# One finishing stage by blocks of token slots, and a pipelined table stage with the edge index in it

## The reference

```python
def _forward(x, edge_index, W_gat, att_src, att_dst, b_gat, ln_gamma, ln_beta, W1, b1, W2, b2):  # x = layernorm(t2)
    h = (x_flat @ W_gat).reshape(M, HEADS, NUM_EXPERTS)              # 4 heads x 4 experts
    src, dst = edges and one loop (m, m) per token
    e = leaky_relu(a_src[src] + a_dst[dst], 0.2)
    ee = exp(e - segment_max(e, dst)[dst])
    alpha = ee / (segment_sum(ee, dst)[dst] + 1e-16)
    agg = segment_sum(h[src] * alpha[:, :, None], dst) + b_gat
    scores = _layernorm(agg, ln_gamma, ln_beta).mean over heads      # 4 scores per token
    topk_s, topk_i = top_k(scores, 2); w = softmax(topk_s)
    for ei in range(4):
        out = out + g_ei[..., None] * (gelu(x @ W1[ei] + b1[ei]) @ W2[ei] + b2[ei])
    return out
# result: t2 + out
```

## Time and profile before

| | us |
|---|---|
| median of 3 runs | 6876.4 |
| lowest and highest | 6873.09, 6878.02 |
| the profiled execution | 6868.53 |
| its span | 6867.0 |
| DVE busy in the span | 3009.2 (44%) |
| POOL busy | 3021.5 (44%) |
| PE busy | 2998.4 (44%) |
| POOL's 2048 gathers of the edge stage, busy | 2008.8 |

### The profile page before, as it was taken

The page is one execution under the profiler, slowest core; times in us unless marked ns, Lnnn a source line. Parts: engine busy times, 40 slices in busy tenths (PEclk is TensorE's granted clock), DMA queues, the critical chain, the costliest instruction groups (busy, mean ns, idle before and its releaser), DMA issues. The chain is left out here.

```text
span 6867.0 us, 61389 instructions
## 1 busy us (share of the span) xinstructions
PE 2998.4 (44%) x16592; PEld 2106.3 (31%) x16592; DVE 3009.2 (44%) x4102; ACT 1471.6 (21%) x5678; POOL 3021.5 (44%) x3316
## 2 busy tenths in 40 slices
PE   2888888879999450000444231313121131314400
PEld 1444454468888340000333120202111120203200
DVE  5888888559999321011999020201111020202229
ACT  0333333468888220000000010100000010101100
POOL 1000000046767237776000767575757667572345
PEclk9788888779999555555555555555555555555555
DMA  6666666556666331000000011111111111111125
GB/s 138 89 92 94 96 95 96 83 90 102 103 101 102 87 91 8 9 7 7 3 4 3 13 46 16 33 24 33 28 32 25 15 46 15 34 24 47 49 70 198
DMA packets 584829, 385.88 MB, mean 56 GB/s; under 512 B 404739, under 2 KB 531507, under 8 KB 581715
## 3 DMA queue, kind: packets, MB, share of 16 engines
q1 hardware_dynamic: 385528, 221.54, 14.5%
q10 hardware_dynamic: 89403, 109.89, 9.2%
q0 software_dynamic: 109728, 52.69, 6.6%
HBM read 235.34 MB, written 147.70 MB: 56 GB/s over the span
## 5 line engine op out<-in xcount | busy, mean ns | idle before, releaser
L1483 POOL DMA_INDIRECT e_row<-scratch_table,e_edge x2048 | 2008.8, 981 | 990.0 <-issue 681.8
L1664 PE MATMUL f_psY<-f_w,f_hid 128*128 128x64 f32 x1568 | 363.1, 425 | 1649.5 <-ACT f_hid L1615 1052.8
L1547 DVE TENSOR_TENSOR f_y<-f_psY,f_b 128x1024 f32<-128x1024 f32 x49 | 59.8, 1220 | 2294.7 <-DMA scratch_vpad<-v 1432.9
L1664 PEld LDWEIGHTS f_psY<-f_w,f_hid 128*128 128x128 f32 x1568 | 342.6, 330 | 1741.9 <-ACT f_hid L1615 1117.1
L1522 DVE TENSOR_TENSOR i_hot<-f_psH,i_digit 128x1024 bf16<-128x1024 f32 x512 | 582.4, 1214 | 639.9 <-DMA scratch_b<-c_b3p 371.6
L1615 ACT ACTIVATE f_hid<-f_psH,f_b 128x512 f32<-128x512 f32 x196 | 131.4, 687 | 2920.5 <-PE f_psH L1659 1352.0
L1647 PE MATMUL f_psH<-i_hot 128*128 128x128 bf16 x2048 | 264.8, 310 | 958.2 <-DVE i_hot L1522 814.5
L947 POOL MEMSET a_wproj<- 128x128 f32 x1 | 0.2, 210 | 1368.4 <-POOLq L144 1368.4
L1060 ACT ACTIVATE prob<-psS,low 128x100 f32<-128x100 f32 x1568 | 514.1, 373 | 62.1 <-DVE low L1093 62.0
L1647 PEld LDWEIGHTS f_psH<-i_hot 128*128 128x128 bf16 x2048 | 197.2, 140 | 1025.7 <-DVE i_hot L1522 879.4
L455 PE MATMUL psH<-h,c_w 128*128 128x448 f32 x1008 | 508.7, 592 | 3.6 <-ACT h L567 1.8
(11 more groups left out here) (280 smaller groups left out, 5385.6 us busy)
## 6 DMA issues: line engine op xcount, KB each, us to landing
stack<-scratch_parts ACTq DMA_DIRECT2D x504, 112.0 KB
e_row<-scratch_table,e_edge POOLq DMA_INDIRECT x2048
scratch_y<-f_y ACTq DMA_DIRECT2D x49, 512.0 KB
g_y<-scratch_y SPq DMA_DIRECT2D x28, 896.0 KB, 4.9
scratch_state<-e_state SPq DMA_DIRECT2D x16, 1536.0 KB, 6.0
val<-scratch_vpad SPq DMA_DIRECT2D x672, 35.0 KB
scratch_parts<-h2p ACTq DMA_DIRECT2D x56, 336.0 KB, 3.8
keys<-scratch_kpad SPq DMA_DIRECT2D x112, 155.0 KB
```

Source lines behind the costliest of these rows:

```text
L1483: pool.indirect_dma_start(out=row[s][:, f, :], out_offset=None, in_=table_dram, in_offset=bass.IndirectOffsetOnAxis(ap=edge[s][:, 0, f:f + ...
L1664: m = pe.matmul(psY[par][:, j, e * C:(e + 1) * C], hid[e][:, j * 128:(j + 1) * 128], w2[:, e, :], start=True, stop=True)
```

## The change

The table stage's block now holds the index work too. The 12 steps of the index work stand in DVE's stream behind 12 of the table's iterations; SP issues their stores ahead of those of the last chunks. The table's 28 chunks are written out instead of looped, with four buffers instead of two, and each engine's stream is shifted between chunks: DVE sums chunk i, inverts chunk i-2, centres i and takes the variance of i-1.

Join and output stage are one block, `finish_phase`. The sums stay on chip in `g_sums`; the store to `scratch_sums` and the reload are gone. Token slots are numbered so that slots 0 to 127 of a partition are tokens with edges and slots 128 to 195 are the others. Gates and mixing go by blocks of slots: 128 to 195 first (no sums needed), then 0 to 47, 48 to 95 and 96 to 127, each of these once its own gathers have landed. Table rows, constants and the first five chunks of `y` and `t2` are loaded at the stage's start. The mixing is by chunks of 8 slots, all on DVE, and sums the experts by two contiguous additions instead of one reduction; POOL issues the gathers and nothing else.

```diff
 # table stage, DVE
-                    dve.tensor_reduce(st(0), t2[par][:], AX.X, ALU.add).then_inc(step, 1)
-                    ...
-                    dve.reciprocal(st(5), st(4)).then_inc(inv_done, 1)
-                every_chunk(dve, layernorm)
+                for i in range(COUNT + 2):          # COUNT = 28, RING = 4 buffers
+                    if i < COUNT: total(i)
+                    if 2 <= i: inverse(i - 2)
+                    if i < COUNT: center(i)
+                    if 1 <= i <= COUNT: variance(i - 1)
+                    if index is not None and 1 <= i <= index.STEPS:
+                        index.step(dve, i - 1)       # the 12 steps of the index stage
 # table stage, POOL / PE / ACT
+                for i in range(COUNT + 2):
+                    if i < COUNT: squares(pool, i)
+                    if 2 <= i: scale(pool, i - 2)
+                for i in range(COUNT + 1):
+                    if i < COUNT: turn(i)            # 7 transposes
+                    if 1 <= i: rows_of(i - 1)        # 7 products
+                for i in range(COUNT + 3):
+                    if 3 <= i: copies(i - 3)
+                    if 2 <= i < COUNT + 2: channels(i - 2)
+                    if i < COUNT: deviation(i)
 # table stage, SP: index.load(sp) first of all; then
+                for k in range(COUNT + 1):
+                    if k + RING < COUNT: load(k + RING)
+                    if k > 0: out(k - 1)
+                    if index is not None and k == COUNT - 2:
+                        index.store(sp)              # 2 MB, 2 small ones, 4 MB
+                ...
+                    index.stored_all(sp)
+        clear(nc, semaphores)

 # join stage, SP
-                sp.wait_ge(sums_in, 16 * 128)
-                sp.dma_start(sums_dram[0:NODES].rearrange("(p t) c -> p t c", p=128), sums[:]).then_inc(sums_out, 16)
-                sp.wait_ge(sums_out, 32)
+                for part, rows_of in slots(table_dram, 0, JT):
+                    sp.dma_start(row[:, part, :], rows_of).then_inc(rows_in, 16)
+                ...                                  # adst, constants
+                for k in range(SLOTS): load(k)       # SLOTS = 5: y and t2
+                for k in range(NCH):                 # NCH = 25
+                    out(k)
+                    if k + SLOTS < NCH: load(k + SLOTS)
 # join stage, POOL
-                pool.wait_ge(sums_out, 16)
-                for t in range(128):
-                    pool.indirect_dma_start(out=sums[:, t, :], ...).then_inc(sums_in, 16)
+                pool.wait_ge(blank, 2)
+                for i, (lo, hi) in enumerate(BLOCKS_AT):   # [(128, 196), (0, 48), (48, 96), (96, 128)]
+                    if lo < NODE_SLOTS:
+                        for t in range(lo, hi):
+                            pool.indirect_dma_start(out=sums[:, t, :], ...).then_inc(sums_in[i], 16)
 # join stage, DVE: the two memsets of sums stand behind the index of the mend instead of first; behind g_fixed:
+                dve.wait_ge(rows_in, ROW_LOADS)
+                def combine(i, lo, hi): ...          # 13 operations; the third waits: sums_in[i], 16 * n
+                def gates(i, lo, hi): ...            # 40 operations, those of the output stage on hi - lo slots
+                def scale(k):
+                    dve.tensor_tensor(scaled[k % 2][:, 0:n], y[s][:, 0:n], gate[:, lo:hi, :].unsqueeze(3).to_broadcast([128, n, EXPERTS, C]), ALU.mult)
+                def halve(k):
+                    dve.tensor_tensor(half[k % 2][:, 0:n], scaled[k % 2][:, 0:n, 0:2, :], scaled[k % 2][:, 0:n, 2:4, :], ALU.add)
+                def whole(k):
+                    dve.tensor_tensor(mix[k % 2][:, 0:n], half[k % 2][:, 0:n, 0, :], half[k % 2][:, 0:n, 1, :], ALU.add)
+                def residual(k):
+                    dve.tensor_tensor(res[s][:, 0:n], mix[k % 2][:, 0:n], t2[s][:, 0:n], ALU.add)
+                for i, (lo, hi) in enumerate(BLOCKS_AT):
+                    if lo < NODE_SLOTS: combine(i, lo, hi)
+                    gates(i, lo, hi)
+                    for k in range(count + 3): ...   # scale k, halve k-1, whole k-2, residual k-3
 # output stage: removed as a stage
-                        dve.tensor_reduce(mix[s % 2][:], scaled[s % 2][:].rearrange("p j e c -> p j c e"), AX.X, ALU.add)
-                        scale(pool, turn, s + 1)
-                        add(turn, s)
-                        add(turn, s + 1)
```

More of the change, by code:

```diff
@@ L139, with slots, spans_of @@
 SORT_FIRST = 44
+SPANS = [(0, 128, 0), (128, JT, NODES)]
+def slots(a, lo, hi):
+    for first, last, token in SPANS:
+        x, y = max(lo, first), min(hi, last)
+        if x < y:
+            part = a[token:token + (last - first) * 128].rearrange("(p j) c -> p j c", p=128)
+            yield slice(x - lo, y - lo), part[:, x - first:y - first, :]
+def spans_of(lo, hi):
+    return sum(1 for first, last, token in SPANS if max(lo, first) < min(hi, last))
 def clear(nc, semaphores):
@@ L1243, in table_phase, with squares @@
+        loads = lambda k: 16 * sum(spans_of(*of(i)) for i in range(k % RING, k + 1, RING))
+        stores = lambda k: 16 * sum(1 + 2 * spans_of(*of(i)) for i in range(k % RING, k + 1, RING))
+        z_view = z_dram[:, at * 128:(at + COUNT * JC) * 128].rearrange("c (k x) -> k c x", k=COUNT)
         PARTS = [(0, 4), (4, JC)]
[L1245 to L1249, removed]
+        def squares(eng, k):
+            r = k % RING
+            eng.wait_ge(cen_done, k + 1)
+            wait(eng, squared, k - RING + 1)
+            eng.tensor_tensor(sq[r][:], cen[r][:], cen[r][:], ALU.mult).then_inc(sq_done, 1)
@@ L1280, in _ @@
+                for r in range(RING):
+                    sp.wait_ge(stored[r], stores(r + (COUNT - 1 - r) // RING * RING))
+                if index is not None:
+                    index.stored_all(sp)
             @block.vector
@@ L1290, in _ @@
                 m.then_inc(weights, 1)
[L1292 to L1300 removed]
+                st = lambda k, j: stat[k % RING][:, j, :]
@@ L2030, in build_program @@
     attention_phase(nc, io, t1, q, kpad, vpad, t2)
-    index_phase(nc, io, ordered, digit, edge, first, ends)
-    table_phase(nc, io, t2, z, table, adst)
+    with ExitStack() as ctx:
+        index = Index(nc, ctx, ctx, ordered, digit, edge, first, ends)
+        table_phase(nc, io, range(N), t2, z, table, adst, index=index)
     edge_phase(nc, io, z, table, adst, digit, edge, node, first, b, state, y)
-    join_phase(nc, io, state, node, first, ends, sums)
-    output_phase(nc, io, table, adst, sums, y, t2, out)
+    finish_phase(nc, io, state, node, first, ends, table, adst, y, t2, out)
 def kernel(**inputs):
```

601 lines of the change are left out of this document (328 added, 273 removed).

## The result

| | before | changed |
|---|---|---|
| median, us | 6875.5 (4 runs, 6873.1 to 6878.0) | 6628.0 (4 runs, 6626.1 to 6631.2) |
| profiled span, us | 6867.0 | 6624.5 |

The account below looks back on a forecast made before the run. No engine was taken as full: stages run in a row and chunks wait for themselves, beside an unedited 3895.0 us edge stage. 6868.5 - 88.6 (table, index) - 119 (finish) = 6660.9, as a median 6669 us, range 6595 to 6735.

Parts of the forecast that it names:

- Table and index: Stages ahead of the edge stage: chunks overlap, PE sets the period, a tail of stores ends it; gain 88.6 us.
- 27 x 4.95 + 3 = 136.7: Table stage: 27 periods of 4.95 us, semaphore gap included, plus 3 us for index operations that make chunks late.
- rival (c): Table stage: PE's clock rises above 0.50, 35 us more gained, 6634 us; chance 0.06.
- Edge stage: The unedited stage between table and finish: 3895.0 us again.
- Rival (d): Edge stage: shifted code and addresses make its gathers take longer, slower than before at 6880 us; chance 0.03.
- Finish: Former join and output stages: gates and mixing partly overlap the gathers, DVE slowed beside them; gain 119 us.
- 53 at 1.4 = 74.2: Finish, slots 0 to 47: 53 small DVE instructions at one per 1.4 us beside gathers, 74.2 us.
- crawl: Finish: beside gathers DVE runs off what is queued, then gets about one instruction per 1.4 us; forecast chance 0.53.
- 36 instructions at 1.4: Finish, first block's mixing: 36 DVE instructions at one per 1.4 us beside gathers, from 6481.6 to 6532.
- stock as 24 instructions: Finish: DVE has some 24 instructions queued to run at full pace before the slow pace sets in.
- rival (a): Finish: no crawl, gates and mixing at full speed beside gathers, gain 176 us, 6612 us; chance 0.20.
- rival (b): Finish: deeper crawl and slower gathers, 128 of them adding 22 us, 6697 us; chance 0.14.

Follow-up runs that it names:

- e5: Changed kernel with the four index stores issued behind the 13th chunk's loads instead of next to last; 6625.8 us, ratio 0.9639.
- e6: Changed kernel with the first five y and t2 loads held until the mended sums are written, and the memsets first again; 6618.9 us, ratio 0.9635.
- e7: Changed kernel with the edits of e5 and e6 together; 6625.6 us, ratio 0.9638.
- e3: Kernel before with 400 small DVE operations added beside the join stage's gathers, 200 in straight code, then 200 in a hardware loop; 6892.5 us.
- e10: Changed kernel with DVE's work of each finish block inside a one-turn hardware loop; 5612.5 us, ratio 0.9581, on the other chip.
- e8: Kernel before with 400 straight small DVE operations held until four gathers have landed; 5853.5 us beside 5857.0, on the other chip.
- e9: Kernel of e8 with POOL clearing a spare tile 60 times ahead of its gathers; 5912.6 us beside 5857.0, on the other chip.
- e4: Changed kernel without the loads of y and t2 behind the first five chunks, later chunks mixed from what the buffers hold; 6613.2 us.
- e11: Changed kernel with the index stores cut into 16 pieces behind the last chunks from the 13th on; 5597.5 us, ratio 0.9566, on the other chip.
- e12: Kernel of e10 run once more, against the changed kernel without the branches; 5607.1 us, ratio 0.9584, on the other chip.

## Why the prediction was right, and where it was not

- **Table and index, 88.6 forecast, 96.3 measured.** Right in mechanism: PE sets the period (no idle time in its rows), first transposes 16.6 us after the start (forecast 16.1), and a tail of stores, 29.2 us from the first of them (2415.3) to the edge stage (forecast 29.9). The size: 130.0 us between the first transposes (2283.94) and the last (2413.95) where 27 x 4.95 + 3 = 136.7 stood, since a full PE needs 4.74 us a chunk and no gap for a semaphore. PE's clock stayed at 0.50 with PE busy for 133 of 177 us, so rival (c) is out; by the Trainium skill ("TensorE: Matmul & The Clock Gate", Part 1: The HAM clock gate) activity should have released it, and this trace disagrees as the one before did.
- **Edge stage.** Unchanged, 3899.0; it was 3892.7 to 3895.2 in e5, e6 and e7, so the 4 us are scatter. Rival (d) is out.
- **Finish, 119 forecast, 147.9 measured. The step that failed is "53 at 1.4 = 74.2".** DVE did not crawl beside these gathers: the window of its combine, gates and mixing of slots 0 to 47 is 57.8 us from 6452.08 to 6509.90, where the forecast had 108. The first block's mixing took 47.0 us where "36 instructions at 1.4" gave 50.4, but by luck: it ran at full pace and waited 7.7 us for `g_t`, which I had costed at nothing, and neither cost time, since the gathers landed later still. The crawl exists (e3, and single scans 1.4 us apart again at 4363.77 to 4366.57 of the changed trace), but I took its stock as 24 instructions. In e3 the supply was 200 operations by 45 us after the first gather, then 0.71 a us, which gives some 212 at 62 us, 266 at 138 us, 318 at 211 us. The finish had used some 76, 153 and 227 busy operations at those points (6434, 6510, 6583; counts of the windows view). It asked for less than e3 was given, so no shortage would show. That the finish takes the same 280 us on the chip without the crawl (e10) shows that the crawl costs nothing there. That stock and rate are the reason fits the counts, but no run tests it: e10's rival, that the finish escapes by its waits or its longer instructions, is open. That the supply in the edge stage is poorer because its stock was used up or dropped long before is only argued as well; e8, e9 and e10 might have told on the first chip. Full supply came back some 11 us behind the last gather in e3, where the forecast estimated 19.
- **What kept rival (a)'s 176 from being reached.** Two terms of my own list that I sized too low: the first gather at 28.3 us, not 22.9 (5.4 us; without the loads and memsets ahead of it it came at 21.8, e6, so they cost 6.5 us instead of 4.7, and 3.5 us more have another source that no run isolates), and gathers at 1.584 us instead of 1.325, 26.6 us until the 96th had landed, of which rival (b) had the mechanism (it priced all 128 at 22 us; they came to 32.9) and e4 shows the cause. From the landing of the 96th to the end it took 98.1 us, 4 less than (a)'s 102, since gate blocks cost 26.5 and 20.3 us, not 29.8 and 24.2, against one wait of 3.1 us for `g_t` in the mixing between them. 5.4 + 26.6 - 4 = 28, the difference between 176 and 147.9. With these the total by (a) is 6612 - 7.7 (table) + 28 = 6632 for a median, beside the 6628 measured.
- The range would have held with either miss alone, since it took in (a) and (b). That 6628 lies only 41 us from the forecast is in part luck: no crawl alone made it 57 us too high, and the late first gather and slower gathers took 28 of that back.

## What to carry to other kernels

A slow pace seen beside some work may be a rate and a stock (e3): before using it elsewhere, compare what the new place asks for in all with stock plus rate times duration, not each instruction with the rate. A large store was no cheaper in the middle of a pipeline whose loads share the queue (21.8 us of stall, 16.7 as a tail, e5); in pieces part of it got beside the chunks (8.7 us, e11). When work is moved beside gathers, ask first what it does to the gathers, since they end last.

## What the runs showed of the hardware

- Two chips ran the kernel before in 6870 and in 5857 us. The change gained 247.5 us where the crawl is, and on the other chip, with the branches of e10 and e12 in it, 244 and 243 us. The difference lies in the edge stage (in the changed kernel 3899.0 against 5334.94 - 2459.51 = 2875.4 us) and comes with the crawl: on the slow one DVE gets down to an instruction per 1.4 us beside gathers (e3), on the fast one 400 of 400 run at full pace (e8). By the Trainium skill ("Runtime: NRT & Kernel Launch", Instruction fetch mechanics) instructions stream in and the cost is mostly hidden: e8 agrees, e3 does not. The duration of an edge-stage gather is nearly the same, 983 ns in the changed kernel and 964 in e10 in the mean, and the granted clock in the edge stage 0.50 in both. Why the chips differ is open.
- A gather of 128 rows takes 1.0 us beside an idle DVE or one with `tensor_scalar` operations of 24 elements (e3: 1.02 at most), and mostly 1.4 to 2.5 us (3.0 at most) beside additions and products of two inputs of 512 to 2048 elements, loads or no loads (e4). Whether the length or the second input does it, no run tells apart.
